# The keys' sums of squares dealt to partitions by a small DMA of ScalarE instead of identity matmuls, layer 0 attention

## The chip, the cores and the metric

The kernel runs on one core of a Trainium2 chip. The metric is the time of one execution on the device in microseconds. Three runs of the kernel before took 1753.96 to 1756.87 us, with a median of 1755.95 us.

## The reference, cut to what matters

The whole is two layers of gated cross attention and feed forward on 4 batches of 256 tokens of width 256. The change lies in layer 0's attention. There, each of 8 groups has one own key and value head and one context key and value head (128 wide), and 2 query heads for each of the two kinds:

```python
k = _fp8_linear_pertensor(ln_out, wk, wk_scale, k_in_scale).reshape(b, s, g, d)
k = _ln(k, kln_w, kln_b)                       # 256 own keys of a batch
kvx = jnp.einsum('bsi,oi->bso', cond, w_kv_x)
kx, vx = jnp.split(kvx, 2, axis=-1)
kx = _ln(kx.reshape(b, sc, g, d), kxln_w, kxln_b)   # 1601 context keys
scores = jnp.einsum('bsghd,btgd->bghst', q, k) * scale
p = jax.nn.softmax(scores, axis=-1)
```

So each of the 1601 + 256 = 1857 keys of a pair (group, batch) has a norm of its own, 1 / sqrt(its sum of squares over 128 + 128 * 1e-5). The kernel centres the weights beforehand, so that the mean is gone, and multiplies the scores by the norms, one number for each column of the score matrix, the same for all 128 queries (partitions).

## The kernel before, in words

The attention loop runs over 32 pairs (`NGB`); in iteration `it` the scores, softmax and values of pair `it` are computed in four blocks of 128 queries (`4 * it` to `4 * it + 3`), beside the projection of keys, values and queries of pair `it + 1`. The loop starts at -1, to fill. In the iterations 0 to 11 (`SPLITS` = 12) the engines also split the weights of a later group. Each engine has its own program, and all are in an order written out by hand; an engine waits only where a semaphore says so, and works strictly in its order.

TensorE's small products go through three PSUM banks by turns, in the order of `SLOTS` (line 801); `bank_of` and `wait_bank` give each product its bank and make it wait until the one three slots before has been read. The slots of one iteration: Q0, K0, K1, TQ0 (query transposes), K2, K3, Q1, SS (sums of squares), V0, ST (their transposes), V1, TQ1, V2, RS with V3 (the norms' transpose, in the free columns of V3's bank) and PR (output projection).

The path of the norms, before:

1. ScalarE writes the squares of the keys into `sq`, 128 x 1857, padded to 1872 = 16 x 117 (L1422).
2. TensorE, `squares` (L1632): four matmuls with a matrix of ones of 32 columns, each of 468 columns of `sq`, one to each quarter of the partitions of the bank.
3. ScalarE, `sums_out` (L1460): a copy to `sqs`.
4. TensorE, `turn_squares` (L1647): four fp32 transposes by the identity, 117 rows each.
5. VectorE, `squares_out` (L1197): takes one column of each quarter and adds the epsilon, to `ssc`, 117 x 16.
6. GpSimd, `key_norm` (L1054): to the power -0.5, to `rr`.
7. TensorE, `turn_norms` (L1720): one transpose, to 16 rows of 117.
8. ScalarE, `norms_out` (L1468): a copy of the 16 rows to `rsr`.
9. SP, `row_out` (L940): a DMA of the 16 rows to HBM, and `row_in` (L948): a DMA that reads the row back to all 128 partitions of `rsb` (in even iterations that buffer lies in the tile `x`).

VectorE needs the row in `scaled` (L1220) at the start of the next iteration, where it multiplies scores and norms and takes the maximum.

SP issues all DMAs of the loop: the weights of coming pairs, the small row and its broadcast, and eight transposing DMAs an iteration (`turn_p`, L962), which turn the probabilities for TensorE's `times_v` (L1765). A transposing DMA waits for VectorE's low part of the probabilities (`p_lo`, L1253) and GpSimd's own part (`split_self`, L1070).

Of the kernel before, what the change touches and what calls it, by code (L numbers as in the profile page):

```python
# [13 lines left out]
P = 128  # L14
# [36 lines left out]
SQG, SQT = 4, 4  # L51
SQW = (KC + SQG * SQT - 1) // (SQG * SQT)
SQN = SQG * SQT
RSC = SQN * SQW

BEFORE = 2 * STAGE + 2 * IC * WCOLS + 2 * RSC + 2 * SQT * SQW + 3 * 1024 + 2 * 2 * NQ * P + 2 * KCOLS + 2 * KTILES * D + 508
# [18 lines left out]
pa_full k_sq k_bias k_lo sums_out ssq_out kr_pow rst_out v_hi v_lo st_done mv_done rs_pow nm_done normed  # L75
# [30 lines left out]
def build(nc, A, out):  # L106
    m = Mem()
    whole = ExitStack()
    with whole:
# [5 lines left out]
        m.rs_d = nc.dram_tensor("rs_d", (2, SQN, SQW), F32, kind="Internal").ap()  # L115
# [9 lines left out]
def allocate(nc, m, whole):  # L125
# [14 lines left out]
    m.ones = sb(whole, "ones", [P, R], F32)  # L140
    m.rsmc = sb(whole, "rsmc", [P, 2 * G * HPG], F32)
# [11 lines left out]
    with ExitStack() as attn:  # L153
# [28 lines left out]
        with ExitStack() as c:  # L182
            m.stage = [sb(c, f"stage{i}", [P, STAGE], BF16) for i in range(2)]
            m.wsb = sb(c, "wsb", [P, 2 * IC * WCOLS], BF16)
            m.sq = sb(c, "sq", [P, RSC], F32)
            m.sqs = sb(c, "sqs", [P, SQT * SQW], F32)
# [6 lines left out]
            sb(c, "free_mid", [P, 254], F32)  # L193
# [15 lines left out]
            m.ssc = sb(c, "ssc", [P, SQN], F32)  # L209
            m.rr = sb(c, "rr", [P, 32], F32)  # L210
            m.rsr = sb(c, "rsr", [32, P], F32)
# [14 lines left out]
        with ExitStack() as c:  # L226
# [14 lines left out]
            m.wg = sb(c, "wg", [P, IC, NE], F32)  # L241
            m.brow = sb(c, "brow", [P, NE], F32)
# [304 lines left out]
def pool_prologue(e, m, s):  # L547
# [9 lines left out]
    e.memset(m.rr[:, :], 0.0).then_inc(s["p_pad"], 1)  # L557
    e.memset(m.sq[:, KC:RSC], 0.0).then_inc(s["p_pad"], 1)
# [234 lines left out]
def pe_prologue(e, m, s):  # L793
# [11 lines left out]
RS0 = 392  # L805
# [81 lines left out]
def wait_bank(e, s, it, what):  # L887
# [6 lines left out]
    if SLOTS[at] == ("PR",) and 0 <= it < LAG:  # L894
        at -= 3
# [3 lines left out]
    if before[0] == "Q":  # L899
        e.wait_ge(s["normed"], 2 * it + int(before[1]) + 1)  # L900
    elif before[0] == "K":
        e.wait_ge(s["k_lo"], 4 * it + int(before[1]) + 1)
    elif before[0] == "T":
        e.wait_ge(s["q_t32"], 2 * it + int(before[2]) + 1)
    elif before == "SS":
        e.wait_ge(s["sums_out"], it + 1)
    elif before == "ST":
        e.wait_ge(s["ssq_out"], it + 1)
    elif before[0] == "V":
        e.wait_ge(s["v_lo"], 4 * it + int(before[1]) + 1)  # L910
        if before == "V3":
            e.wait_ge(s["rst_out"], it + 1)
    else:
        e.wait_ge(s["acc_done"], it - LAG + 1)


def sp_attention(e, m, s):
# [22 lines left out]
    def row_out(it):  # L940
        if not it < NGB:
            return
        e.wait_ge(s["rst_out"], it + 1)
        if it >= 2:
            e.wait_ge(s[f"rs_in{it % 2}"], 16 * (it // 2))
        e.dma_start(m.rs_d[it % 2], m.rsr[0:SQN, 0:SQW]).then_inc(s["rs_row"], 16)

    def row_in(it):  # L948
# [10 lines left out]
        e.dma_start(m.rsb[it % 2], m.rs_d[it % 2].rearrange("t k -> (t k)").partition_broadcast(P)).then_inc(  # L959
# [17 lines left out]
    for it in range(-1, NGB + LAG - 1):  # L977
# [32 lines left out]
        row_out(it + 1)  # L1010
        if it < NGB:
# [3 lines left out]
        row_in(it + 1)  # L1015
# [13 lines left out]
def pool_attention(e, m, s):  # L1029
# [24 lines left out]
    def key_norm(it):  # L1054
        if not it < NGB:
            return
        e.wait_ge(s["ssq_out"], it + 1)
# [46 lines left out]
    for it in range(-1, NGB + LAG - 1):  # L1104
# [39 lines left out]
def dve_attention(e, m, s):  # L1144
# [51 lines left out]

    def squares_out(it):  # L1197
        if not it < NGB:
            return
        e.wait_ge(s["pa_full"], made(it, "ST"))  # L1200
        if it:
            e.wait_ge(s["kr_pow"], it)
        sums = bank_of(m, "ST")[0:SQW, :].rearrange("p (t g r) -> p g t r", t=SQT, g=SQG)[:, :, :, 0]
        e.tensor_scalar(m.ssc[0:SQW, :].rearrange("p (g t) -> p g t", g=SQG), sums, D * EPS5, None,  # L1204
                        ALU.add).then_inc(s["ssq_out"], 1)
# [91 lines left out]
    for it in range(-1, NGB + LAG - 1):  # L1297
# [53 lines left out]
        squares_out(it + 1)  # L1351
# [54 lines left out]
def act_attention(e, m, s):  # L1406
# [53 lines left out]
    def sums_out(it):  # L1460
# [7 lines left out]
    def norms_out(it):  # L1468
        if not it < NGB:
            return  # L1470
        e.wait_ge(s["pa_full"], made(it, "V3"))
        if it:
            e.wait_ge(s["rs_row"], 16 * it)
        e.copy(m.rsr[0:SQN, 0:SQW], bank_of(m, "RS")[0:SQN, RS0:RS0 + SQW]).then_inc(s["rst_out"], 1)

# [32 lines left out]
    for it in range(-1, NGB + LAG - 1):  # L1508
        if it == 0:
            e.wait_ge(s["p_pad"], 4)  # L1510
# [40 lines left out]
        sums_out(it + 1)  # L1551
# [28 lines left out]
        norms_out(it + 1)  # L1580
# [18 lines left out]
def pe_attention(e, m, s):  # L1599
# [32 lines left out]
    def squares(it):  # L1632
# [6 lines left out]
        if it == 0:  # L1639
            e.wait_ge(s["p_pad"], 2)  # L1640
# [4 lines left out]
        r.then_inc(s["pa_full"], 1)  # L1645

    def turn_squares(it):  # L1647
        if not it < NGB:
            return
        bank = bank_of(m, "ST")  # L1650
        wait_bank(e, s, it, "ST")
        e.wait_ge(s["sums_out"], it + 1)
        for t in range(SQT):
# [1217 lines left out]
```

## Time and profile before

| | |
|---|---|
| median of 3 runs | 1755.95 us (1753.96 to 1756.87) |
| profiled execution | 1757.05 us, span 1755.3 us |
| TensorE matmul busy | 1623.6 us, 92% of the span |
| VectorE, ScalarE, GpSimd busy | 80%, 79%, 72% |
| granted TensorE clock, mean | 0.974 |

A row of a timeline shows when an instruction (or a few of the same kind, "x4") started, counted from the span's start, and how long it took; in brackets stands how long its engine had been idle and what ended that. Matmuls overlap, so that the time a group takes in TensorE's order is read from its start to the start of the next group. A granted clock of 1.00 is TensorE's upper level. PE is TensorE, DVE VectorE, ACT ScalarE, POOL GpSimd, SP SyncE, and "SPq" is SP's queue, whose rows for a DMA give the time of the issue, not of the transfer. The loop's first iteration with scores begins near 100 us, its last products of keys and values end near 1165 us.

### The profile page before, as it was taken

To read this page: it belongs to the slowest core of one execution; us is meant where nothing else is said; L and a number is where in the kernel's file an instruction comes from. 1 tells how busy PE (TensorE), PEld (TensorE's weight loads), DVE (VectorE), ACT (ScalarE), POOL (GpSimd) and SP (SyncE) were. 2 spreads that over 40 slices of the span, in tenths; PEclk is the share of its full clock that TensorE was granted. 3 is DMA by queue.
4 is the path that set the end of the run, shared out by engine and by line. 5 is a ranking of instruction groups with operands and counts; after the bars stand their busy time and mean duration, and the time that the engine had idled before them with its cause. 6 is when DMAs were issued, how large, how long until landed. Compare 5 with 4: busy or idle time off the path is not lost. (4 is left out here: it accounts for less than half of the span.)

```text
span 1755.3 us, 43546 instructions
## 1 busy us (share of the span) xinstructions
PE 1623.6 (92%) x15989; PEld 1032.1 (59%) x16182; DVE 1405.2 (80%) x3479; ACT 1385.0 (79%) x2333; POOL 1272.2 (72%) x1171
## 2 busy tenths in 40 slices
PE   3389999999999999999999999998898999999997
PEld 1256776777677767777777777766553333333332
DVE  8879999999998898889988888888995755545322
ACT  4388888988887788778878887874346999999996
POOL 3646787787877876778777777775897989979500
PEclk9589999999999999999999999999999999999998
DMA  4269999999998889999999999997424222212100
GB/s 171 87 130 187 183 193 215 207 203 208 199 210 181 201 179 195 205 211 200 194 185 201 226 198 195 196 196 156 149 47 106 44 49 71 43 32 44 32 14 13
DMA packets 603173, 261.37 MB, mean 149 GB/s; under 512 B 568784, under 2 KB 575952, under 8 KB 601552
## 3 DMA queue, kind: packets, MB, share of 16 engines
q1 hardware_dynamic: 602960, 258.57, 70.7%
q8 instruction: 129, 2.11, 0.5%
q14 instruction: 84, 0.69, 0.1%
HBM read 99.15 MB, written 17.28 MB: 66 GB/s over the span
## 5 line engine op out<-in xcount | busy, mean ns | idle before, releaser
L1781 PE MATMUL pv<-PT,VV 128*128 128x256 bf16 (+1 forms) x2880 | 340.7, 275 | 7.7 <-DMA PT<-PB 7.6
L2351 POOL TENSOR_TENSOR l_rr<-l_rr,mhalf 128x32 f32<-128x32 f32 (+1 forms) x60 | 332.7, 5545 | 5.0
L1761 PE MATMUL score<-KK,QT 128*128 128x512 bf16 (+2 forms) x1795 | 315.5, 318 | 12.6 <-DVE mxp L1238 5.0
L1781 PEld LDWEIGHTS pv<-PT,VV 128*128 128x128 bf16 (+1 forms) x2880 | 280.7, 99 | 75.1 <-issue 33.7
L1505 ACT ACTIVATE PB<-S,rsum 128x1024 bf16<-128x1024 f32 (+1 forms) x256 | 246.3, 987 | 84.9 <-DVE rsum L1269 80.4
L1260 DVE SCALAR_TENSOR_TENSOR PB<-S,rsum,PB 128x1024 bf16<-128x1024 f32 (+1 forms) x256 | 302.4, 1182 | 1.9 <-ACT PB L1505 1.9
L1761 PEld LDWEIGHTS score<-KK,QT 128*128 128x128 bf16 x1920 | 159.7, 98 | 143.6 <-DVE mxp L1238 11.6
L1495 ACT ACTIVATE S<-S,nmx 128x1601 f32<-128x1601 f32 x128 | 209.8, 1639 | 10.2 <-DVE nmx L1250 10.1
L2617 ACT ACTIVATE P<-score 128x1024 f32<-128x1024 f32 x196 | 199.1, 1060 | 11.6 <-PE score L2709 5.9
L2729 PE MATMUL pv<-P,V 128*9 128x256 f32 (+1 forms) x2288 | 154.4, 385 | 2.8 <-ACT P L2617 2.2
L1621 PE MATMUL tb<-stage,wsb 128*128 128x512 bf16 x767 | 148.8, 337 | 5.5 <-DVE stage L624 4.1
L1079 POOL TENSOR_SCALAR S<-S,rsum 128x256 f32<-128x256 f32 x128 | 65.0, 508 | 115.1 <-DVE rsum L1269 102.8
L1062 POOL TENSOR_TENSOR rr<-ssc,mhalf 117x16 f32<-117x16 f32 x32 | 93.2, 2914 | 47.3 <-DVE ssc L1204 47.3
L1101 POOL TENSOR_TENSOR catq<-yt,ym 128x512 bf16<-128x512 f32 x64 | 120.6, 1884 | 0.3
L1238 DVE CUSTOM_DVE_ANT_0 S<-score,x 128x1024 f32<-128x1024 f32 (+1 forms) x128 | 104.5, 816 | 14.3 <-PE score L1761 11.8
L1238 DVE CUSTOM_DVE_ANT_0 S<-score,rsb 128x1024 f32<-128x1024 f32 (+1 forms) x128 | 104.5, 817 | 14.0 <-PE score L1761 9.8
L1621 PEld LDWEIGHTS tb<-stage,wsb 128*128 128x128 bf16 x768 | 67.0, 99 | 70.9 <-issue 8.7
L1035 POOL TENSOR_SCALAR a_nm<-a_mv 128x4 f32<-128x4 f32 x64 | 42.3, 661 | 89.8 <-DVE a_mv L1194 89.8
L1445 ACT ACTIVATE kn<-pa,a_nm,a_rs 128x128 f32<-128x128 f32 x256 | 95.9, 458 | 13.6 <-POOL a_nm L1040 13.6
L1417 ACT ACTIVATE KK<-tb,dcols 128x512 bf16<-128x512 f32 (+1 forms) x128 | 76.3, 596 | 37.0 <-PE tb L1621 35.8
L1083 POOL TENSOR_TENSOR PB<-S,PB 128x256 bf16<-128x256 f32 x128 | 96.6, 755 | 10.9
L1673 PE MATMUL tb<-wsb,stage 128*128 128x128 bf16 x1536 | 99.0, 222 | 4.5 <-DVE KK L1161 4.5
(271 smaller groups left out, 3627.7 us busy)
## 6 DMA issues: line engine op xcount, KB each, us to landing
x<-rs_d SPq DMA_DIRECT2D x16, 936.0 KB, 6.8
rsb<-rs_d SPq DMA_DIRECT2D x16, 936.0 KB, 5.5
wsb<-w_split SPq DMA_DIRECT2D x46, 256.0 KB, 4.5
wsb<-w_split SPq DMA_DIRECT2D x23, 512.0 KB, 5.4
wpr<-in_wprojT SPq DMA_DIRECT2D x23, 512.0 KB, 3.9
context_d<-stage SPq DMA_DIRECT2D x16, 400.2 KB, 3.7
l_ctx<-context_d SPq DMA_DIRECT2D x4, 1601.0 KB, 7.4
rawh<-in_w_all SPq DMA_DIRECT2D x12, 512.0 KB, 5.4
```

The source lines that it names most:

```text
L1101: e.tensor_tensor(out[:, :, pr * 256:(pr + 1) * 256], m.yt[:, :].rearrange("p (k c) -> p k c", k=2), m.ym[pr][:, :].rearrange("p (k c) -> ...
L1238: e.tensor_tensor_reduce(m.S32[par][:, at:at + b - a], m.score[:, a:b], m.rsb[it % 2][:, key:key + b - a], 1.0, start, ALU.mult, ALU.max, ...
L1260: e.scalar_tensor_tensor(m.PB[n % 2][:, lo:lo + b - a], m.S32[n % 2][:, a:b], m.rsum[n % 2][:, 1:2], m.PB[n % 2][:, 2 * a:a + b], ALU.mult ...
L1495: e.activation(x, x, ACT.Exp, bias=m.nmx[par][:, 1:2], accum_out=m.sums[par][:, 1:2])
L1505: e.activation(m.PB[n % 2][:, 2 * a:a + b], m.S32[n % 2][:, a:b], ACT.Copy, scale=m.rsum[n % 2][:, 1:2]).then_inc(s["p_hi"], 1)
L1621: r = e.matmul(bank[:, 0:b - a], wk[:, w, ic, D:2 * D], ctx_op(m, it, part, ic, a, b), start=(n == 0), stop=(n == 5))
L1673: r = e.matmul(bank[:, h * D:(h + 1) * D], ctx_op(m, it, part, ic, t * P, (t + 1) * P), wv[:, w, ic, D:2 * D], start=(n == 0), stop=(n == 5))
L1761: i = e.matmul(m.score[:, at:at + b - a], qt[:, kind, qp, q * P:(q + 1) * P], kk[:, kp, a:b], start=(k == 0), stop=(k == 2))
L1781: i = e.matmul(m.pv[:, at:at + 256], vv[0:rows, v, t, :], m.PT[k % 2][0:rows, turned(c, a), :], start=(c == first and r == 0), stop=(c == ...
L2351: e.tensor_tensor(rr, rr, m.mhalf[0:rows, 0:NH1], ALU.pow).then_inc(s["l1_rr"], 1)
L2617: e.activation(pr[:, :], bank, ACT.Exp, scale=float(D1) ** -0.5).then_inc(s["l1_exp"], 1)
L2729: r = e.matmul(m.pv[j * R:j * R + VC, 0:S], m.V1[p][0:rows, t, 4 * hq + j, :], probabilities(m, n, j // 2)[0:rows, at:at + S], start=(t == ...
```

## The change

The padded row gets another form: 1857 keys are padded to 1920 = 128 x 15. The four matmuls of the sums take 480 columns each. ScalarE's copy adds the epsilon, and ScalarE then waits for that copy and issues a DMA from four partitions of `sqs` (one of each quarter, 480 numbers) to all 128 partitions of `ssc` (15 numbers each). GpSimd raises these to the power -0.5, and SP sends `rr` (128 x 15) straight to HBM, of which the first 1872 numbers (`RSC`) are read back to all partitions, as before. The steps 4, 5, 7 and 8 above go, and with them the slots ST (left empty) and RS.

The order changes in three places: ScalarE takes the sums out ahead of the first part of the probabilities of block `4 * it + 1` (from iteration 0 on); GpSimd's `key_norm` comes after `split_self(4 * it + 1)`; SP's `row_in` comes directly behind `row_out`, ahead of the load of the projection's weights. Two small tiles (`wg`, `brow`) move to another place in SBUF, and the unused space is adjusted.

```diff
-SQG, SQT = 4, 4
-SQW = (KC + SQG * SQT - 1) // (SQG * SQT)
-SQN = SQG * SQT
-RSC = SQN * SQW
+SQG = 4
+SQC = (KC + P - 1) // P
+SQW = P * SQC // SQG
+RSC = KC + 15
...
-SLOTS = (("Q0",), ("K0",), ("K1",), ("TQ0",), ("K2",), ("K3",), ("Q1",), ("SS",), ("V0",), ("ST",), ("V1",), ("TQ1",),
-         ("V2",), ("RS", "V3"), ("PR",))
+SLOTS = (("Q0",), ("K0",), ("K1",), ("TQ0",), ("K2",), ("K3",), ("Q1",), ("SS",), ("V0",), (), ("V1",), ("TQ1",), ("V2",),
+         ("V3",), ("PR",))
...
-    if SLOTS[at] == ("PR",) and 0 <= it < LAG:
+    if not SLOTS[at] or SLOTS[at] == ("PR",) and 0 <= it < LAG:
         at -= 3
...
# SP
-        e.wait_ge(s["rst_out"], it + 1)
+        e.wait_ge(s["kr_pow"], it + 1)
         if it >= 2:
             e.wait_ge(s[f"rs_in{it % 2}"], 16 * (it // 2))
-        e.dma_start(m.rs_d[it % 2], m.rsr[0:SQN, 0:SQW]).then_inc(s["rs_row"], 16)
+        e.dma_start(m.rs_d[it % 2], m.rr[:, :]).then_inc(s["rs_row"], 16)
...
         row_out(it + 1)
+        row_in(it + 1)
         if it < NGB:
             load_projection(it - 1)
         if it == NGB - 1:
             load_projection(NGB - 1)
-        row_in(it + 1)
...
# GpSimd
-        e.wait_ge(s["ssq_out"], it + 1)
+        e.wait_ge(s["sums_in"], 16 * (it + 1))
         if it:
-            e.wait_ge(s["pa_full"], made(it - 1, "RS"))
-        else:
-            e.wait_ge(s["p_pad"], 1)
-        e.tensor_tensor(m.rr[0:SQW, 0:SQN], m.ssc[0:SQW, :], m.mhalf[0:SQW, 0:SQN], ALU.pow).then_inc(s["kr_pow"], 1)
+            e.wait_ge(s["rs_row"], 16 * it)
+        e.tensor_tensor(m.rr[:, :], m.ssc[:, :], m.mhalf[:, 0:SQC], ALU.pow).then_inc(s["kr_pow"], 1)
...
+        split_self(4 * it + 1)
         key_norm(it + 1)
         if it == -1:
             pool_round_end(e, m, s, 5)
-        split_self(4 * it + 1)
...
# ScalarE, sums_out
         if it:
-            e.wait_ge(s["pa_full"], made(it - 1, "ST"))
-        e.copy(m.sqs[:, :], bank_of(m, "SS")[:, 0:SQT * SQW]).then_inc(s["sums_out"], 1)
+            e.wait_ge(s["sums_in"], 16 * it)
+        e.activation(m.sqs[:, :], bank_of(m, "SS")[:, 0:SQW], ACT.Copy, bias=D * EPS5).then_inc(s["sums_out"], 1)
+        e.wait_ge(s["sums_out"], it + 1)
+        if it:
+            e.wait_ge(s["kr_pow"], it)
+        e.dma_start(m.ssc[:, :], m.sqs[0:SQG * R:R, :].rearrange("j (r c) -> j r c", c=SQC)).then_inc(s["sums_in"], 16)
...
# ScalarE, order of the loop
         exponentials(4 * it + 1)
         for b, i in SPLIT_AT.get(it, ())[0:1]:
             act_piece_high(e, m, s, b, i)
+        if it >= 0:
+            sums_out(it + 1)
         p_hi(4 * it + 1, 0)
         query_norm(it + 1, 1)
...
-        sums_out(it + 1)
+        if it == -1:
+            sums_out(0)
         values_high(it + 1, 0)
...
         values_high(it + 1, 2)
-        norms_out(it + 1)
         exponentials(4 * it + 2)
...
# TensorE, squares and order of the loop
-        w = SQT * SQW
         for j in range(SQG):
-            r = e.matmul(bank[j * R:(j + 1) * R, 0:w], m.ones[:, :], m.sq[:, j * w:(j + 1) * w], start=True, stop=True,
-                         skip_group_check=True)
+            r = e.matmul(bank[j * R:(j + 1) * R, 0:SQW], m.ones[:, :], m.sq[:, j * SQW:(j + 1) * SQW], start=True,
+                         stop=True, skip_group_check=True)
...
         values(it + 1, 0)
-        turn_squares(it + 1)
         scores(4 * it + 2, 1)
         values(it + 1, 1)
         turn_queries(it + 1, 1)
         values(it + 1, 2)
-        turn_norms(it + 1)
         values(it + 1, 3)
```

The functions `squares_out`, `norms_out`, `turn_squares` and `turn_norms` go as a whole, and so do the waits for them.

## Rows read from the trace of the kernel before

**Rows 1.** The page, DMA queues: packets, MB, share of 16 engines' span

```profile
q1 hardware_dynamic: 602960, 258.57, 70.7%
```

**Rows 2.** Busy times by stretch, the loop's first 12 iterations and the rest

```profile
core 0: us, PE busy (x) PEld busy (x) DVE busy (x) ACT busy (x) POOL busy (x), PEclk, DMA share, GB/s
140.20:526.50 386.30, 379.59 (x3432) 279.08 (x3477) 363.59 (x935) 331.74 (x673) 305.16 (x347) 1.00 0.98 201
526.50:1154.90 628.40, 621.00 (x5639) 461.27 (x5711) 559.92 (x1440) 508.91 (x920) 480.58 (x542) 1.00 0.97 198
```

**Rows 3.** Waits of TensorE in the whole span: total, times, longest

```profile
PE pv L1781 <- DMA PT<-PB: 7.6, 6, 2.7
...
PE tb L1726 <- POOL rr L1062: 1.3, 3, 0.5
...
PE pa L1654 <- ACT sqs L1466: 1.1, 3, 0.4
```

**Rows 4.** Timeline of TensorE in a second-half iteration: start, length, line

```profile
702.66 0.99 PE L1643 MATMUL tb<-sq,ones 128*32 128x468 f32 x8
...
705.90 1.50 PE L1673 MATMUL tb<-wsb,stage 128*128 128x128 bf16 x24
707.24 0.65 PE L1654 MATMUL pa<-ident,sqs 128*117 128x128 f32 x4
707.93 1.02 PE L1761 MATMUL score<-KK,QT 128*128 128x512 bf16 x8
...
710.13 0.61 PE L1717 MATMUL tb<-ident,kn 128*128 128x128 f32 x4
...
711.91 0.27 PE L1726 MATMUL tb<-ident,rr 117*32 117x117 f32 x1
712.02 0.61 PE L1681 MATMUL tb<-wsb,stage 128*128 128x128 bf16 x8
```

**Rows 5.** Timeline of ScalarE, the same stretch

```profile
703.51 1.15 ACT L1505 ACTIVATE PB<-S,rsum 128x1024 bf16<-128x1024 f32 x1 [0.23 <-DVE rsum L1269]
704.57 1.49 ACT L1445 ACTIVATE kn<-pa,a_nm,a_rs 128x128 f32<-128x128 f32 x4
705.94 0.56 ACT L1466 COPY sqs<-tb 128x468 f32<-128x468 f32 x1
707.44 0.59 ACT L1432 CAST VV<-tb 128x512 bf16<-128x512 f32 x1 [0.94 <-PE tb L1673]
```

**Rows 6.** Timelines of VectorE and GpSimd, the same stretch

```profile
708.05 0.69 DVE L1174 TENSOR_TENSOR VV<-tb,VV 128x512 bf16<-128x512 f32 x1
...
710.95 0.69 DVE L1174 TENSOR_TENSOR VV<-tb,VV 128x512 bf16<-128x512 f32 x1 [0.79 <-ACT VV L1432]
...
708.17 2.90 POOL L1062 TENSOR_TENSOR rr<-ssc,mhalf 117x16 f32<-117x16 f32 x1 [2.04 <-DVE ssc L1204]
```

**Rows 7.** DMA issues of lines 974 and 946 from 300 to 1100 us (ns), and SP's timeline

```profile
L974 SPq DMA_TRANSPOSE PT<-PB x184: 1296/2440/5573, 299.5 to 1098.5; - x184
...
DMA to landing us min/median/max: 4.0/5.0/10.0
...
L946 SPq DMA_DIRECT2D rs_d<-rsr x23: 317/326/529, 328.4 to 1096.2; - x23
...
DMA to landing us min/median/max: 1.3/1.8/2.8
...
704.29 6.72 SPq L974 DMA_TRANSPOSE PT<-PB  x3
713.27 0.32 SPq L946 DMA_DIRECT2D rs_d<-rsr  x1
...
714.92 0.32 SPq L959 DMA_DIRECT2D x<-rs_d  x1
```

**Rows 8.** Timelines in a first-half iteration: ScalarE, VectorE, TensorE

```profile
323.25 0.59 ACT L1432 CAST VV<-tb 128x512 bf16<-128x512 f32 x1 [0.42 <-PE tb L1673]
...
303.52 0.08 DVE L1238 DVE_READ_ACCUMULATOR2_ANT mxp<- 128x1 f32 x1
...
303.66 1.47 PE L1761 MATMUL score<-KK,QT 128*128 128x512 bf16 x6
```

More of the change, by code:

```diff
@@ L74 @@
 ld_k ld_q ld_v ld_xq rs_row rs_in0 rs_in1
-pa_full k_sq k_bias k_lo sums_out ssq_out kr_pow rst_out v_hi v_lo st_done mv_done rs_pow nm_done normed
+pa_full k_sq k_bias k_lo sums_out sums_in kr_pow v_hi v_lo st_done mv_done rs_pow nm_done normed
 q_hi q_t32 q_lo pw_in pw_last pw_hi pw_lo acc_done
@@ L140, in allocate @@
     m.ones = sb(whole, "ones", [P, R], F32)
+    m.wg = sb(whole, "wg", [P, IC, NE], F32)
+    m.brow = sb(whole, "brow", [P, NE], F32)
     m.rsmc = sb(whole, "rsmc", [P, 2 * G * HPG], F32)
@@ L184, in allocate @@
             m.wsb = sb(c, "wsb", [P, 2 * IC * WCOLS], BF16)
-            m.sq = sb(c, "sq", [P, RSC], F32)
-            m.sqs = sb(c, "sqs", [P, SQT * SQW], F32)
+            m.sq = sb(c, "sq", [P, SQG * SQW], F32)
+            m.sqs = sb(c, "sqs", [P, SQW], F32)
             m.kn = [sb(c, f"kn{i}", [P, 512], F32) for i in range(2)]
@@ L192, in allocate @@
             vv[0] = sb(c, "VV0", [P, 2, KTILES, D], BF16)
-            sb(c, "free_mid", [P, 254], F32)
+            sb(c, "free_mid", [P, 194], F32)
             qt[1] = sb(c, "QT1", [P, 2, 2, NQ * P], BF16)
@@ L208, in allocate @@
             m.anm = [sb(c, f"a_nm{i}", [P, 4], F32) for i in range(2)]
-            m.ssc = sb(c, "ssc", [P, SQN], F32)
-            m.rr = sb(c, "rr", [P, 32], F32)
-            m.rsr = sb(c, "rsr", [32, P], F32)
+            m.ssc = sb(c, "ssc", [P, SQC], F32)
+            m.rr = sb(c, "rr", [P, SQC], F32)
             m.mxp = [sb(c, f"mxp{i}", [P, 1], F32) for i in range(2)]
@@ L556, in pool_prologue @@
     i.then_inc(s["rank_done"], 1)
-    e.memset(m.rr[:, :], 0.0).then_inc(s["p_pad"], 1)
-    e.memset(m.sq[:, KC:RSC], 0.0).then_inc(s["p_pad"], 1)
+    e.memset(m.sq[:, KC:SQG * SQW], 0.0).then_inc(s["p_pad"], 1)
     e.wait_ge(s["mhalf_done"], 1)
@@ L1195, in query_stats @@
         mv.then_inc(s["mv_done"], 1)
[L1197 to L1205, printed above, removed]
     def projected(i):
@@ L1464, in sums_out @@
         if it:
-            e.wait_ge(s["pa_full"], made(it - 1, "ST"))
-        e.copy(m.sqs[:, :], bank_of(m, "SS")[:, 0:SQT * SQW]).then_inc(s["sums_out"], 1)
[L1468 to L1471, printed above, removed]
+            e.wait_ge(s["sums_in"], 16 * it)
+        e.activation(m.sqs[:, :], bank_of(m, "SS")[:, 0:SQW], ACT.Copy, bias=D * EPS5).then_inc(s["sums_out"], 1)
+        e.wait_ge(s["sums_out"], it + 1)
         if it:
-            e.wait_ge(s["rs_row"], 16 * it)
-        e.copy(m.rsr[0:SQN, 0:SQW], bank_of(m, "RS")[0:SQN, RS0:RS0 + SQW]).then_inc(s["rst_out"], 1)
+            e.wait_ge(s["kr_pow"], it)
+        e.dma_start(m.ssc[:, :], m.sqs[0:SQG * R:R, :].rearrange("j (r c) -> j r c", c=SQC)).then_inc(s["sums_in"], 16)
     def projection_high(i):
@@ L1509, in act_attention @@
         if it == 0:
-            e.wait_ge(s["p_pad"], 4)
+            e.wait_ge(s["p_pad"], 3)
             e.wait_ge(s["w_lo_dve"], 16)
@@ L1639, in squares @@
         if it == 0:
-            e.wait_ge(s["p_pad"], 2)
-        w = SQT * SQW
+            e.wait_ge(s["p_pad"], 1)
         for j in range(SQG):
-            r = e.matmul(bank[j * R:(j + 1) * R, 0:w], m.ones[:, :], m.sq[:, j * w:(j + 1) * w], start=True, stop=True,
-                         skip_group_check=True)
[L1645 to L1653, printed above, removed]
-            r = e.transpose(bank[0:SQW, t * P:(t + 1) * P], m.sqs[:, t * SQW:(t + 1) * SQW], m.ident[:, :])
+            r = e.matmul(bank[j * R:(j + 1) * R, 0:SQW], m.ones[:, :], m.sq[:, j * SQW:(j + 1) * SQW], start=True,
+                         stop=True, skip_group_check=True)
         r.then_inc(s["pa_full"], 1)
@@ L1661, in values @@
         bank = bank_of(m, f"V{i}")
-        if i < 3:
-            wait_bank(e, s, it, f"V{i}")
+        wait_bank(e, s, it, f"V{i}")
         if i == 0:
@@ L1718, in turn_queries @@
         r.then_inc(s["pa_full"], 1)
-    def turn_norms(it):
-        if not it < NGB:
-            return
-        bank = bank_of(m, "RS")
-        wait_bank(e, s, it, "RS")
-        e.wait_ge(s["kr_pow"], it + 1)
-        e.transpose(bank[0:R, RS0:RS0 + SQW], m.rr[0:SQW, :], m.ident[0:SQW, 0:SQW]).then_inc(s["pa_full"], 1)
     def project(i):
@@ L1940, in pe_turn_tokens @@
         e.wait_ge(s["v_lo"], 4 * NGB)
-        e.wait_ge(s["rst_out"], NGB)
     elif k == 2:
```

16 lines of the change are left out of this document (4 added, 12 removed).

## The prediction, made before the changed kernel ran

> **What bounds the kernel now.** I read the page for its DMA queue first [rows 1], then the busy times by stretch, then the waits of TensorE, and only then the timelines of one iteration. In the attention loop's second half (526.5 to 1154.9 us) it is busy 621.0 of 628.4 us, in its first half (140.2 to 526.5 us) 379.6 of 386.3, both at a granted clock of 1.00, the upper level (2.4 GHz) [rows 2]. VectorE stands at 559.9 of 628.4 in the second half (89%) but at 363.6 of 386.3 in the first (94%); ScalarE at 81% and 86% [rows 2]. So inside the loop a microsecond of TensorE's own work is a microsecond of time, unless another engine has less room than what is saved, and that can only be so in the first half. The waits of TensorE agree: at the two groups that go, it waited 1.1 and 1.3 us in the whole run, and for the transposed probabilities 7.6 us [rows 3]. The iteration shown starts its squares at 702.66 us.
>
> **TensorE, removed.** The four transposes of the sums start at 707.24, the next matmul group (scores) at 707.93: 0.69 us of the order of work. The one transpose of the norms starts at 711.91, the values' last piece at 712.02: 0.11 us, though the row gives its own length as 0.27, since it overlaps its neighbours [rows 4]. Together 0.80 us an iteration. **Added:** the squares' sums run over 480 columns in place of 468. Their eight records last 0.99 us, so 12/468 of that, 0.02 us. Net 0.78 us.
>
> **VectorE and ScalarE, removed.** VectorE's small addition (117 by 16) and ScalarE's copy of the 16 rows both go. Both engines have idle time right behind them (VectorE 0.79 us at 710.95 [rows 6]), so I count them as nothing; they are room in hand.
>
> **ScalarE, added and moved.** The copy of the sums (0.56 us) comes before the probabilities' first part and the four query norms instead of after them, and carries the DMA issue behind it. TensorE's squares end at 703.65 (702.66 + 0.99) [rows 4]; ScalarE's exponentials are done before 703.51, where it starts the part after an idle 0.23 us [rows 5]. So the copy runs 703.7 to 704.3. Then it waits for its own result and issues the transfer. No DMA is issued by ScalarE in this trace, so I bound the issue from both sides: 0.32 us is the plain DMA on SP (the row's minimum 317 ns, maximum 529), and 2.44 us is the median of a transposing one on the same queue, 5.57 its longest [rows 7]. I take 0.32, since the nearest row is that of a plain DMA of the same small row; with 0.1 us for the wait on itself (an estimate: a bit more than twice the 0.04 us from the end of TensorE's V0, 705.90 + 1.50 [rows 4], to its copy at 707.44 [rows 5]) ScalarE is free at 704.7. The probabilities' part, which started at 703.51, starts 1.2 us later; the four norms then end at 707.2 in place of 706.06 [rows 5]. What hides this: until now the copy (0.56) and an idle 0.94 us before the values' copy at 707.44 followed [rows 5], and that copy waits for TensorE's V0, which isn't moved. Who waits for the norms: TensorE's query transposes at 710.13, after the change 709.44 [rows 4]: 2.2 us of room. They also need V0's low part out of their bank, done at 708.74 (708.05 + 0.69) [rows 6]: 0.7 us of room, plus the 0.2 us that ScalarE is early at V0. So an issue of up to 0.32 + 0.9 = 1.2 us costs TensorE nothing in this iteration; beyond that each microsecond costs one.
>
> **The transfer and the row behind it.** Landing is bounded by 1.3 us (the least of the small row to HBM, 1.8 in the median) and 10.0 us (the longest of a transposed block, 5.0 in the median) [rows 7]. I take 3 us, nearest the small one: 704.6 to 707.6. GpSimd's power, on it, ran from 708.17 to 711.07 after 2.04 us of idling for VectorE's sums [rows 6]. In the new order GpSimd first does the own-keys split, which fits into that idle time (its inputs have long been there), and starts the power at about 707.9: 15 columns by 2.90/16 each make 2.72 us, done at 710.6. The row's DMA, at 713.27 until now behind TensorE's transpose and ScalarE's copy, goes at 710.7, the broadcast at about 712.7 instead of 714.92 [rows 7]. SP's queue: the projection's load is moved behind the broadcast, and the transposes of the second probability half stand behind both; all of them get earlier. The transfer may land 2.2 us later than I take it (5.2 us in all) before even the row is later than now. The wait for the earlier round's row is met an iteration before. The broadcast stays at 1872 numbers. The added small packets load the DMA engines: 602,960 packets took 70.7% of 16 engines' 1755 us, 33 ns each [rows 1]; some 256 small ones in place of 16 are 0.5 us an iteration for each engine. TensorE hardly waits for DMA, so I cost it at nothing; if the cover were gone it would be that 0.5 us, 15 us in all.
>
> The trace gives 1.8 us for a transfer whose 16 rows lie on as many partitions [rows 7]. The Trainium skill, "DMA: Bandwidth & Descriptors", section "Why a DMA increments its semaphore by 16 and not by 1", states that a DMA is spread over the largest number of engines, at most 16, that divides the slowest dimension of both sides. Here these are 4 and 128, so four engines would take 32 packets each; by the 33 ns above that is an estimated 1.1 us on top of 1.8. By the row alone the landing is at 1.8 us, by the rule at 2.9, and the sum is the same by both, since 5.2 would be hidden.
>
> **What is late next.** In the second half: VectorE idles 0.79 us for V1's copy alone [rows 6], so it keeps up with 0.78 us. I take all of it: 19 iterations by 0.78 are 14.8 us. In the first 12 (those that also split weights) ScalarE ends its weight work at 322.83 and then idles 0.42 us for V1 at 323.25 [rows 8]; with V1 0.69 us earlier it is ScalarE that is late, so V1's copy moves by about 0.5. From there VectorE works nearly without a gap into the next iteration, where TensorE's scores at 303.66 start just after VectorE's last read at 303.52 + 0.08 [rows 8]. So those iterations follow V1's copy: 12 by 0.5 are 6.0 us. The fill iteration ahead of the loop has long stalls of its own: nothing. The waits at the two groups [rows 3], 2.4 us, go in part: 1.2. Sum 22.0 us. Profiled execution: 1757.05 us (span 1755.3 and 1.75 around it) minus 22.0 is 1735.05. It lies 1.1 us above the median of the runs, 1755.95, so in the median's terms 1734.
>
> **The rivals.**
> Something else holds part of it: VectorE, at 94% in the first half, gives nothing there, and the 0.5 us of packets shows in some of the rest. For: the tight step at 303.66. Against: VectorE loses work as well. First half 0 (6.0 us less), second half 19 by 0.5 in place of 0.78 (5.3 less): 1745.
> ScalarE's issue is held up. At 704.29, just when it issues, SP starts three transposing DMAs, 6.72 us [rows 7]. If ScalarE's is held for as long as the shorter of them lasts (1.3 to 1.5 us, so 1.5), the second half loses 0.3 of its 0.78 us (19 by 0.48 are 9.1 gained), while in the first half all of 1.2 us over my 0.32 comes through, 12 by (1.2 - 0.5) are 8.4 lost; with the waits' 1.2 that is 2 us gained: no change that can be told, 1754. This is the case within 0.2%. The skill's same page, section "Issuing engines are not separate DMA queues", states that they all run on the same 16 engines and interleave, and that only the sequencer's time is saved; it puts no price on waiting. No run here shows it.
> The other side, slower: the same place at the median price of a transpose, 2.44 us. Second half: 2.44 is 1.24 over the free 1.2, minus 0.78 leaves 0.46 lost, by 19 are 9 us; first half 2.1 - 0.5 = 1.6 by 12, 19 us; less the waits' 1.2 that is plus 27, 1783. It decides from an issue of about 1.6 us on. For it: the transposes really meet it every iteration. Against: plain DMAs on SP take 0.32 to 0.53 us even right behind transposes. A landing near 10 us would do it too, over the row: power at 714.6, row 717.3, broadcast 719.2, more than 4 us later than now.
> That the change doesn't do what it says (the sums not needed by TensorE any more, but its banks still waited for): the values' third bank now waits for the query norms of Q1, done before; I give it nothing.
>
> **How the numbers follow.** Forecast 0.57 (1734, its own range 1727 to 1741: below, 31 by 0.80 and all waits, 28 us; above, two thirds of the 22 us), part held 0.14 (1745), no change 0.11 (1754), slower 0.18 (1783 and up). A measurement can tell 0.2%, 3.5 us, from no change. Faster 0.71, same 0.11, slower 0.18. The range 1726 to 1762 leaves out most of the slower case and little below.
>
> **What would show it.** Right: iterations of the second half at 33.8 to 33.9 us; no transposes between V0 and the scores; ScalarE's gap between the sums' copy and the next part under 0.6 us; GpSimd's power starting before V0's low part ends; the row's DMA some 2.5 us earlier. Wrong: a gap of over 1.5 us on ScalarE behind the copy, the query transposes waiting for VectorE's V0 part, GpSimd idling for the small transfer past 710 us of such an iteration, or TensorE idle in front of the scores for VectorE's maximum in every iteration.

## The result, and the profile after

The changed kernel takes 1736.43 us (median of 4 runs, 1733.42 to 1740.90) against 1756.07 us (4 runs) for the kernel before: ratio 0.9888, 95% interval 0.9872 to 0.9904. So the gain is 19.6 us, with 1734 forecast and a range from 1726 to 1762. The profiled execution took 1734.62 us (span 1732.8), 22.4 less than the profiled one of before.

The busy times of the two parts of the loop, which answer to [rows 2] (same stretches of the clock, so a little more work falls into each):

```profile
140.20:526.50 386.30, 381.16 (x3500) 278.27 (x3498) 363.03 (x931) 333.65 (x668) 310.92 (x351) 1.00 0.96 203
526.50:1154.90 628.40, 624.04 (x5714) 458.56 (x5712) 560.33 (x1444) 513.08 (x917) 502.09 (x552) 1.00 0.98 201
```

TensorE seems nearer to full than before (624.0 of 628.4 us against 621.0), but this difference comes from the records. The trace of the kernel before lacks 125 matmuls of the scores (1795 are recorded for 1920 weight loads), and this trace of the changed kernel lacks none. A second trace of the same changed kernel (the run `e0_after` below) lacks as many and shows 620.0 of 628.4. What can be said is that in a plain second-half iteration (one without an extra wait) of the complete trace TensorE has no idle time. First this trace, then the incomplete one of the same kernel:

```profile
900.00:934.06 34.06, 34.06 (x315) 25.04 (x313) 29.87 (x80) 27.92 (x51) 27.16 (x30) 1.00 1.01 205
...
692.18:726.24 34.06, 33.85 (x312) 25.05 (x312) 29.85 (x80) 28.05 (x51) 27.19 (x31) 1.00 0.98 189
```

TensorE's timeline of such an iteration, answering to [rows 4]:

```profile
692.18 1.01 PE L1621 MATMUL tb<-sq,ones 128*32 128x480 f32 x8
...
695.44 1.50 PE L1640 MATMUL tb<-wsb,stage 128*128 128x128 bf16 x24
696.78 1.24 PE L1720 MATMUL score<-KK,QT 128*128 128x512 bf16 x9
...
699.19 0.61 PE L1684 MATMUL tb<-ident,kn 128*128 128x128 f32 x4
...
726.24 1.01 PE L1621 MATMUL tb<-sq,ones 128*32 128x480 f32 x8
```

The next squares start 34.06 us later; before, it was 34.62 us (the squares' starts at 702.66 [rows 4] and 737.28). So a second-half iteration is 0.57 us shorter (34.62 to 34.05, in nearly all of them). A first-half one is 0.53 us shorter (34.94 to 34.41, again the commonest values). From the first squares to the last, the loop is 17.9 us shorter in the profiled pair: 10.2 us over the last 18 intervals, 8.8 over the 12 before them (2.8 of these in the one right behind the fill), and the fill itself 1.1 us longer. The 2.8 us are no sure gain of the change: that one interval took 37.8 us before and 35.0 after, but from 36.7 to 37.7 in five of the later variants of the changed kernel, and 35.9 in the kernel before with more transposes. The remaining 4.5 us of that pair lie behind the last squares. That part isn't touched by the change, and over the profiles of this case it took between 595.4 and 601.6 us, without relation to the kernel. So the totals of single executions can differ by some 6 us from there alone, and the size of an effect is better read from the iterations than from the totals.

ScalarE and its queue, SP's queue and GpSimd in the same iteration, answering to [rows 5], [rows 7] and [rows 6]; "ACTq" is the issue of the DMA:

```profile
693.26 0.57 ACT L1447 ACTIVATE sqs<-tb 128x480 f32<-128x480 f32 x1 [0.47 <-PE tb L1621]
693.86 0.53 ACTq L1451 DMA_DIRECT2D ssc<-sqs  x1
694.50 1.15 ACT L1482 ACTIVATE PB<-S,rsum 128x1024 bf16<-128x1024 f32 x1 [0.66 <-ACT sqs L1447]
695.55 1.49 ACT L1426 ACTIVATE kn<-pa,a_nm,a_rs 128x128 f32<-128x128 f32 x4
...
693.80 8.36 SPq L968 DMA_TRANSPOSE PT<-PB  x3
702.25 0.53 SPq L940 DMA_DIRECT2D rs_d<-rr  x1
704.47 0.32 SPq L953 DMA_DIRECT2D x<-rs_d  x1
...
695.74 0.48 POOL L1071 TENSOR_SCALAR S<-S,rsum 128x256 f32<-128x256 f32 x1
696.29 1.49 POOL L1073 CAST PB<-S 128x256 bf16<-128x256 f32 x1
697.86 0.67 POOL L1075 TENSOR_TENSOR PB<-S,PB 128x256 bf16<-128x256 f32 x1
698.49 2.75 POOL L1054 TENSOR_TENSOR rr<-ssc,mhalf 128x15 f32<-128x15 f32 x1
```

The issue on ScalarE takes 0.53 us and leaves a gap of 0.66 us, although SP starts its three transposing DMAs 0.06 us ahead of it. Here GpSimd doesn't wait for the transfer: its split of the own keys fills the time until 698.49. In the 31 iterations with scores it waited once, 2.5 us, when the power started only 7.2 us behind the issue.

### The profile page after: what moved, and what is told of

Its sections match the earlier page's. It is cut to its first block and busy times, and to the rows that moved or that the text cites. A ratio compares the mean times of both kernels' runs of the same rounds, so it can differ in the third digit from the quotient of the medians.

```text
span 1732.8 us, 43279 instructions
## 1 busy us (share of the span) xinstructions
PE 1619.0 (93%) x16022; PEld 1014.7 (59%) x16022; DVE 1389.3 (80%) x3447; ACT 1377.3 (79%) x2301; POOL 1284.1 (74%) x1170
## 5 line engine op out<-in xcount | busy, mean ns | idle before, releaser
L1720 PE MATMUL score<-KK,QT 128*128 128x512 bf16 (+2 forms) x1920 | 341.9, 322 | 6.2 <-DVE mxp L1220 5.0
L1242 DVE SCALAR_TENSOR_TENSOR PB<-S,rsum,PB 128x1024 bf16<-128x1024 f32 (+1 forms) x256 | 295.4, 1154 | 4.6 <-ACT PB L1482 4.5
L1600 PE MATMUL tb<-stage,wsb 128*128 128x512 bf16 (+1 forms) x768 | 150.3, 339 | 4.8 <-DVE stage L623 4.1
L1083 POOL TENSOR_TENSOR yt<-yq,ym 128x512 f32<-128x512 bf16 x64 | 95.9, 1498 | 13.9 <-DVE ym L1276 9.5
L1426 ACT ACTIVATE kn<-pa,a_nm,a_rs 128x128 f32<-128x128 f32 x256 | 95.5, 454 | 12.3 <-POOL a_nm L1034 12.3
L2664 PE MATMUL score<-QB,KT 32*128 32x256 bf16 (+1 forms) x1110 | 93.6, 275 | 7.3 <-ACT P L2572 4.8
```

Of the source, the lines that this page charges most:

```text
L1242: e.scalar_tensor_tensor(m.PB[n % 2][:, lo:lo + b - a], m.S32[n % 2][:, a:b], m.rsum[n % 2][:, 1:2], m.PB[n % 2][:, 2 * a:a + b], ALU.mult ...
L1600: r = e.matmul(bank[:, 0:b - a], wk[:, w, ic, D:2 * D], ctx_op(m, it, part, ic, a, b), start=(n == 0), stop=(n == 5))
L1720: i = e.matmul(m.score[:, at:at + b - a], qt[:, kind, qp, q * P:(q + 1) * P], kk[:, kp, a:b], start=(k == 0), stop=(k == 2))
L2664: r = e.matmul(bank[0:rows, at:at + S], m.KT1[p][j * R:(j + 1) * R, hq, t * P:t * P + rows], m.QB[p][j * R:(j + 1) * R, hq, :], start=True ...
```

## The experiments

The iterations given are the distances from one start of the squares to the next, as in the rows above.

**The changed kernel again,** without an edit.

> The changed kernel once more, beside the others of this call. Its first four executions spread from 1733.4 to 1740.9 us, so its gain is known only to about 3 us. Both theories below say 19 to 22 us under the kernel before (the iterations of the second half were 0.57 us shorter in its profile, those of the first half 0.53). If its iterations are the same and the total differs again by some microseconds, the spread lies outside the attention loop.

Measured: 1738.07 us against 1756.89, ratio 0.9891 [0.9875, 0.9907], with the same iterations of 34.05 us. The experiments below are compared with this run. The later ones did not run beside it, so their distances in us to the changed kernel are uncertain by 3 to 6 us.

This trace lacks matmul records, and the profiled one of the result doesn't. The same stretch of the same kernel reads, first in this trace, then in that one:

```profile
695.05 1.50 PE L1640 MATMUL tb<-wsb,stage 128*128 128x128 bf16 x24
696.61 1.02 PE L1720 MATMUL score<-KK,QT 128*128 128x512 bf16 x8
...
695.44 1.50 PE L1640 MATMUL tb<-wsb,stage 128*128 128x128 bf16 x24
696.78 1.24 PE L1720 MATMUL score<-KK,QT 128*128 128x512 bf16 x9
```

Where the scores have 8 records they seem to start 1.56 us behind the group before them, and where they have 9, 1.34 us.

**The four transposes twice, in the kernel before.**

```diff
-        for t in range(SQT):
+        for t in (*range(SQT), *range(SQT)):
             r = e.transpose(bank[0:SQW, t * P:(t + 1) * P], m.sqs[:, t * SQW:(t + 1) * SQW], m.ident[:, :])
```

> The kernel before, with the four transposes of the sums issued twice. Theory A (the bound is TensorE's order; my 0.69 us for the four was too large by one score matmul, 0.21 us, whose record is missing in that trace, so that the four are worth 0.44 to 0.48 us): second-half iterations of 35.06 to 35.11 us in place of 34.62, in all 14 to 15 us more than before, about 1770. Theory B (the four are worth 0.69 us as I read it, and 0.21 us of the gain are lost again to a wait in the changed kernel): 35.3 us, 21 us more, 1777. Theory C (the gain comes from the shorter path of the norms and from the new order, not from TensorE's work): under 3 us more.

Measured: 1765.54 us, ratio 1.0049 [1.0037, 1.0062] to the kernel before. The squares of two successive iterations on TensorE:

```profile
916.30 0.99 PE L1643 MATMUL tb<-sq,ones 128*32 128x468 f32 x8
...
951.35 0.99 PE L1643 MATMUL tb<-sq,ones 128*32 128x468 f32 x8
```

The two shown are 35.05 us apart; the commonest value is 35.06, 0.44 more than 34.62. So four more transposes cost 0.44 us, not 0.69: theory A, as to the iteration. Its total was too high. The first-half iterations of 34.94 us got 0.44 us longer, but the mean over the 11 behind the first was only 0.27, and the fill and the iteration behind it got shorter, hence 9 us in all instead of 14.

**Five transposes back, in the changed kernel.**

```diff
         wait_bank(e, s, it, f"V{i}")
+        if i == 2:
+            for t in range(4):
+                e.transpose(bank[0:117, t * P:(t + 1) * P], m.ident[:, 0:117], m.ident[:, :])
+            e.transpose(bank[0:R, 0:117], m.ident[0:117, 0:R], m.ident[0:117, 0:117])
```

> The changed kernel, with five fp32 transposes of the identity, of the shapes of those that went, put back on TensorE ahead of the values' third group, into a bank that this group overwrites: no other engine reads them, and no wait comes with them. Theory A: 0.54 to 0.58 us an iteration come back, 17 to 18 us, nearly the time of the kernel before (about 1753), second-half iterations at 34.6. Theory B: 0.80 us, but 0.21 us of wait are covered then, so the same. Theory C: within 3 us of the changed kernel.

Measured: 1748.04 us, ratio 0.9954 [0.9942, 0.9967]. Timeline of TensorE:

```profile
905.97 1.01 PE L1621 MATMUL tb<-sq,ones 128*32 128x480 f32 x8
...
940.57 1.01 PE L1621 MATMUL tb<-sq,ones 128*32 128x480 f32 x8
```

Second-half iterations of 34.59 us: 0.54 of the 0.57 us are back, by TensorE's work alone. In the first half 34.59 too, 0.18 more than 34.41, since there TensorE had a wait that took in the rest. So of the total only 10 us came back, not 17. The other 9 us of the gain stayed. In part that follows from where the transposes were put: behind V1, so that V1 was still early and only TensorE's own order got longer. With the transposes at their old place the first half wasn't tested.

**The three moves undone.**

```diff
# ScalarE: behind query_norm(it + 1, 1), as before
-        if it >= 0:
-            sums_out(it + 1)
...
+        sums_out(it + 1)
         values_high(it + 1, 0)
# GpSimd
+        key_norm(it + 1)
...
         split_self(4 * it + 1)
-        key_norm(it + 1)
# SP: row_in(it + 1) behind load_projection again
```

> The changed kernel with its three moves undone: ScalarE takes the sums out and issues after the query norms, GpSimd's power comes ahead of its own-keys split, SP's broadcast comes behind the projection's load. Theory A: the moves only give room; the row is some 2 us later than in the changed kernel, which was not waited for: within 3 us of the changed kernel, second-half iterations at 34.05 to 34.1. Theory C: the moves carry the gain, 10 us or more are lost. A rival within A: GpSimd now waits for the small transfer with the split behind it, the transposing DMA of the second probability half is late, and TensorE waits for it: 0.3 us or more an iteration.

Measured: 1778.51 us, ratio 1.0123 [1.0109, 1.0137]: 40 us over the changed kernel and 22 over the kernel before. My theory A was wrong by 37 us. Waits from 530 to 1130 us (total, times, longest), and then the timelines of one iteration (squares at 647.75) on ScalarE's queue, GpSimd and VectorE:

```profile
POOL rr L1054 <- DMA ssc<-sqs: 68.2, 17, 5.7
DVE S L1220 <- POOL PB L1075: 38.7, 17, 3.8
...
PE score L1717 <- DVE mxp L1220: 15.8, 14, 2.3
...
651.76 0.55 ACTq L1451 DMA_DIRECT2D ssc<-sqs  x1
...
655.65 2.74 POOL L1054 TENSOR_TENSOR rr<-ssc,mhalf 128x15 f32<-128x15 f32 x1 [4.32 <-DMA ssc<-sqs]
...
659.53 0.67 POOL L1075 TENSOR_TENSOR PB<-S,PB 128x256 bf16<-128x256 f32 x1
...
660.23 1.22 DVE L1220 CUSTOM_DVE_ANT_0 S<-score,rsb 128x1024 f32<-128x1024 f32 x1 [2.18 <-POOL PB L1075]
```

The transfer is there 3.9 us behind its issue. GpSimd waits 4.3 us with the split behind it in its order, the split ends 12.4 us behind the squares, and VectorE, which may overwrite that score tile only then, is 2.2 us late; TensorE waits for its maximum in the end. The two runs that follow undo one move each. SP's move wasn't undone alone, and no run has the other two undone without it; in this run the broadcast of the iteration shown still starts 12.1 us behind the squares, against 12.3 in the changed kernel.

**ScalarE's move alone undone** (the first part of the diff above).

> The changed kernel, where only ScalarE's part goes back to its old place (behind the query norms). The transfer was seen to land about 3.5 us after its issue, which is now 2.6 us later, so GpSimd waits some 1.5 us for it, but with its own-keys split already done. Theory D (the 40 us of the old order come from one chain: late transfer, GpSimd waiting for it with the split stuck behind, VectorE waiting for the split before it may overwrite the probabilities): nothing of that chain is left, within 3 us of the changed kernel, second-half iterations at 34.05 to 34.1, GpSimd waiting 1 to 2 us each. Theory E (the place on ScalarE alone costs, since the later parts of the probabilities get late): 10 us or more over the changed kernel.

Measured: 1740.54 us, ratio 0.9909 [0.9877, 0.9940]; second-half iterations of 34.05 us in 9 of 18 cases, GpSimd waiting:

```profile
POOL rr L1054 <- DMA ssc<-sqs: 26.8, 16, 3.3
```

Five first-half iterations that take 34.41 us in the changed kernel take 34.13 to 34.22 here. So the new place of ScalarE's copy costs something in the first half, which I haven't explained.

**GpSimd's move alone undone** (the second part).

> The changed kernel, where only GpSimd's power goes back ahead of the own-keys split. Theory D: the transfer is issued early and lands 3.5 us later, near 697.4 in an iteration whose squares start at 692.2; the power then ends near 700.2 and the split near 701.9, that is 9.7 us after the squares, against 10.7 in the kernel before, where nobody waited. So within 5 us of the changed kernel, second-half iterations at 34.05 to 34.3. Rival F (GpSimd's order alone makes the 40 us): most of them appear here, iterations near 35.2.

Measured: 1743.59 us, ratio 0.9923 [0.9895, 0.9951]; 34.05 us too in most of the second half. GpSimd waits 30.3 us in 16 cases from 530 to 1130 us, but for an early transfer, so in most iterations the split is still in time (VectorE waits for it five times, 7.7 us in all). With one of the two moves undone, 2 and 6 us over the changed kernel are left of the 40, and the intervals of both runs overlap that of the changed kernel. That is what theory D says: one chain, which each of these two moves cuts.

**A second issue on ScalarE.**

```diff
         e.dma_start(m.ssc[:, :], ...).then_inc(s["sums_in"], 16)
+        if it == NGB - 1:
+            return
+        if it:
+            e.wait_ge(s["spare"], 16 * it)
+        e.dma_start(m.scr[:, 0:SQC], m.sqs[0:SQG * R:R, :].rearrange("j (r c) -> j r c", c=SQC)).then_inc(s["spare"], 16)
```

> The changed kernel, with a second DMA of the same form behind the first on ScalarE, into a spare tile that nobody reads. It takes some 0.55 us more of ScalarE's time at the same place (the issue took 0.53 to 0.58 us there). By the prediction's step (up to 1.2 us of issue are free in the second half, none in the first): second-half iterations unchanged at 34.05, first-half ones 0.4 to 0.55 us longer, in all 5 to 7 us. Rival: the issue has no room in either half, 17 us more. Other rival: the issue is a mere gap that the other engines hide everywhere, under 1 us.

Measured: 1743.91 us, ratio 0.9914 [0.9884, 0.9944], 6 us over the changed kernel, which the total alone wouldn't show clear of its spread. The iterations do: the second half stays at 34.05 us, as forecast, and the first half is 6.1 us longer in sum. Nine of its twelve iterations got longer, by 0.1 to 1.1 us. One of them, at 34.41 in the changed kernel, takes 35.27:

```profile
278.98 1.01 PE L1627 MATMUL tb<-sq,ones 128*32 128x480 f32 x8
...
314.25 1.01 PE L1627 MATMUL tb<-sq,ones 128*32 128x480 f32 x8
```

**The power twice on GpSimd.**

```diff
+        e.tensor_tensor(m.scr[:, 0:SQC], m.ssc[:, :], m.mhalf[:, 0:SQC], ALU.pow)
         e.tensor_tensor(m.rr[:, :], m.ssc[:, :], m.mhalf[:, 0:SQC], ALU.pow).then_inc(s["kr_pow"], 1)
```

> The changed kernel, with the power computed twice on GpSimd, first to a spare tile: the row and all behind it on GpSimd come 2.75 us later. By the prediction's step (room of about 2.2 us up to the old place of the row, and none of TensorE's waits on it even there) the time hardly moves: 0 to 0.3 us an iteration, at most 9 us in all. Rival (the earlier row and the earlier GpSimd work carry part of the gain): 0.5 us or more an iteration, 15 us and more.

Measured: 1770.47 us, ratio 1.0075 [1.0044, 1.0106], 32 us over the changed kernel: the rival. The row itself got late in some iterations: VectorE waited for its broadcast in 5 of the 17 from 530 to 1130 us, 8.2 us in all. In a plain one it did not (the row's DMA at 938.05, squares at 925.85), and that one is 0.44 us longer all the same: what stands behind the power on GpSimd has a price that I had not seen. VectorE and GpSimd of this run:

```profile
938.21 1.08 DVE L1272 TENSOR_SCALAR yq<-yq 128x512 bf16<-128x512 bf16 x1
939.32 0.58 DVE L1274 TENSOR_SCALAR ye<-yq 128x512 int16<-128x512 int16 x1
939.94 1.20 DVE L1277 TENSOR_SCALAR ym<-ye 128x512 int16<-128x512 int16 x1
...
937.99 1.15 POOL L1084 TENSOR_TENSOR yt<-yq,ym 128x512 f32<-128x512 bf16 x1
939.09 0.67 POOL L1043 CAST QT<-t 128x512 bf16<-128x512 f32 x1
939.84 1.16 POOL L1045 TENSOR_TENSOR QT<-t,QT 128x512 bf16<-128x512 f32 x1
```

In the changed kernel GpSimd is done with these at 704.57, and the same three of VectorE follow in 0.29 us each:

```profile
703.41 1.16 POOL L1045 TENSOR_TENSOR QT<-t,QT 128x512 bf16<-128x512 f32 x1
...
704.54 0.29 DVE L1271 TENSOR_SCALAR yq<-yq 128x512 bf16<-128x512 bf16 x1
704.87 0.29 DVE L1273 TENSOR_SCALAR ye<-yq 128x512 int16<-128x512 int16 x1
705.19 0.29 DVE L1276 TENSOR_SCALAR ym<-ye 128x512 int16<-128x512 int16 x1
```

Three 0.29 us instructions take 2.9 us when they run against GpSimd's. The inverse sums on VectorE and ScalarE's next part stand behind them, and TensorE waits 0.26 us for VectorE's maximum in this iteration (34.49 us), up to 1.5 in the first half. How the 32 us divide between this and the late row wasn't tested.

**SP issues the small transfer**, ahead of its transposing DMAs, and in another run behind two of them.

```diff
# SP
+        if it >= 0:
+            deal_out(it + 1)      # the waits and the dma_start that stood on ScalarE
         turn_p(4 * it, 1)
         turn_p(4 * it, 0)
# ScalarE issues only the first one itself
...
```

> The changed kernel, where from iteration 0 on SP issues the small transfer instead of ScalarE, ahead of its transposing DMAs of that stretch (the very first one stays on ScalarE). ScalarE loses the 0.66 us between the copy of the sums and the next part. Theory G (the issue on ScalarE costs only where ScalarE has no room, the first half; in the second TensorE has no idle time left): first-half iterations 0.15 to 0.25 us shorter (34.2 to 34.3), second-half ones still 34.05, in all 2 to 3 us under the changed kernel, about 0.987 of the kernel before. Rival H: the transposing DMAs come 0.5 us later and the transfer lands later among them, GpSimd waits for it, and 3 us or more are lost. This is also the version that could beat both.

> The same, but with SP's issue behind two transposing DMAs, each of which holds SP's queue for 1.5 to 4 us. The transfer is then issued some 4 to 5 us later and lands near 10 to 11 us behind the start of the squares; the power and all behind it on GpSimd are 3 to 4 us late, more than in the run with the second power. Theory G: as there or worse, 0.4 to 1.3 us an iteration, 15 to 40 us over the changed kernel. Rival: only the row is late, and it has room since the broadcast is needed 12 us later: under 5 us.

Measured ahead: 1736.93 us, 0.9897 [0.9878, 0.9915], no difference to the changed kernel; behind: 1764.58 us, 1.0042 [1.0009, 1.0074]. Of theory G the run with the late issue is as forecast (27 us over the changed kernel, GpSimd waiting 52.9 us in 16 cases). The first half of the other is not: its iterations stay at 34.42 instead of 34.2 to 34.3, so ScalarE's 0.66 us had cost nothing there either. The issue of the same transfer on SP is of the same length as on ScalarE (from 530 to 1130 us, ns, least, median, most):

```profile
L940 SPq DMA_DIRECT2D ssc<-sqs x17: 561/567/582, 556.3 to 1105.6; - x17
```

**The values' third part ahead of the weight work,** in the order of ScalarE and VectorE.

```diff
# ScalarE; VectorE's values_low(it + 1, 2) moves in the same way
+        values_high(it + 1, 2)
         if 0 <= it < SPLITS:
             act_weights_high(e, m, s, it // 2 + 2, 3 * (it % 2))
         if 0 <= it < SPLITS and it % 2 == 0:
             act_centre_weights(e, m, s, it // 2 + 2)
-        values_high(it + 1, 2)
```

> The changed kernel, where in the first-half iterations ScalarE and VectorE do the values' third part before the weight work of that slot instead of after it. Theory I (what keeps the first half at 34.42 instead of 34.05 us is the stretch from V1 over ScalarE's 3.4 us of query and weight work to V2's low part on VectorE, behind which VectorE has no idle time until TensorE waits for its maximum): the first-half iterations lose 0.1 to 0.35 us each, second-half ones stay at 34.05, in all 1 to 4 us. Rival J: VectorE's total work is the limit there, whatever its order: the first half stays at 34.42 or gets longer.

Measured: 1736.50 us, 0.9881 [0.9859, 0.9904]. Four of the first-half iterations that stood at 34.41 now take 34.05:

```profile
279.67 1.01 PE L1621 MATMUL tb<-sq,ones 128*32 128x480 f32 x8
...
313.72 1.01 PE L1621 MATMUL tb<-sq,ones 128*32 128x480 f32 x8
```

So the place was right for these four (theory I). But the one behind the fill took 37.7 us in place of 35.0, where TensorE waited 3.0 us for a transposed probability instead of 1.9, two of the second half got longer too, and the total doesn't move.

**Both together:** this order, and the small transfer issued by SP ahead of its transposing DMAs.

> The run before together with SP's issue ahead of its transposing DMAs. With SP's issue alone the first half stayed at 34.42 us. Theory I: once the values' third part no longer waits, the 0.66 us on ScalarE may show: 0 to 0.1 us an iteration less than in the run before, not measurable in the total (under 1.5 us). Rival J: no difference to the changed kernel.

Measured: 1735.90 us, 0.9876 [0.9853, 0.9899], the same again, as its rival J has it for the total, though three first-half iterations are at 34.05. No version of these beats the changed kernel by more than the spread.

## Why the prediction was right

**TensorE is the bound** held in the second half: the complete trace has no idle time left in its plain iterations, and 0.54 of 0.57 us come back with the transposes alone.

**The size of the removed work** is the term that was off: net 0.78 us, where 0.57 was measured. In all that is 14.8 us forecast for the second half and 10.2 measured; 0.8 us of that difference is that I counted 19 iterations, and there are 18 distances. I read the four transposes from the start of their group to the start of the scores' [rows 4], 0.69 us. But that scores' group has 8 matmuls in the row and 9 in the changed kernel. One of them, 0.21 us, has no record, and so the group seemed to start late. The two traces of the changed kernel show it without any transposes: 1.56 us with 8 records, 1.34 with 9. 0.69 - 0.21 is 0.48, and the doubling measured 0.44. The single transpose, 0.11, was about right (0.54 - 0.44 = 0.10).

**The first half** came out at 0.53 us an iteration with 0.5 forecast, and 6.0 us over 11 iterations. The twelfth, behind the fill, added 2.8 us that no step of mine explains and that most variants of the changed kernel don't repeat. For the mechanism, that these iterations follow V1's path over ScalarE to VectorE, the run with the values ahead of the weight work speaks, in four iterations; the run with ScalarE's move undone says that the path isn't the whole of it. My reason for 0.5 was wrong: I let V1 come 0.69 us earlier and ScalarE hold it back to 0.5. V1 came only some 0.48 us earlier, and ScalarE's idle 0.42 was all but enough for that. Two errors met in the right figure, which is luck. There was also just enough room for one issue: the second one shows in most first-half iterations.

**ScalarE's issue** took 0.53 us in place of 0.32, with the gap at 0.66 in place of 0.4. That was within the room of 1.2 us that I had worked out for the second half. With the second issue the gap is 1.26 us and more and the iteration still 34.05, so the room is at least that. The rivals of a held-up issue fall: the least and the median in the run are 529 and 548 ns, and only the first of all took 1093.

**The transfer** takes 4.1 us in the median to where GpSimd can use it, 2.4 to 5.5 in the 31 waits of the old order (taken: 3), in time but for the once in the changed kernel, in an iteration of 34.50 us. The Trainium skill, "DMA: Bandwidth & Descriptors", section "Why a DMA increments its semaphore by 16 and not by 1", states besides the number of engines that each of them ends its share with a write to the semaphore. This can be checked on the page's queue row of the changed kernel:

```profile
q10 hardware_dynamic: 4224, 0.25, 0.2%
```

That is 132 packets for each of 32 transfers, 128 of data and 4 more, one for each of four engines; by that rule, the trace agrees.

**The row behind it** was a wrong step that cost nothing. I had the power start before V0's low part ends and the row's DMA and the broadcast go 2.5 and 2.2 us earlier. The power starts 6.31 us behind the squares (before: 5.51) and 0.2 us after V0's low part has ended. The split ahead of it took 2.75 us, its cast alone 1.49, where I had let it fit into 2.04. Then SP's transposing DMAs hold the queue to 702.16. So the row's DMA goes 10.07 us behind the squares (before: 10.61), and the broadcast 12.29 (before: 12.26), not earlier at all. Of my five signs of being right only one came true as written, the transposes gone; the iteration (34.05 for 33.8 to 33.9) and ScalarE's gap (0.66 for under 0.6) missed narrowly, the power's start and the row's DMA clearly. The signs of being wrong stayed away, except that GpSimd did wait once, and TensorE's query transposes three times for VectorE (7.4 us), as they had before the change (5.7).

**"The three moves only give room"** was not a step of the prediction, but what it implied, and what I expected of the old order. The price lies in what GpSimd does next (the split), and, 2.75 us later than now, in GpSimd's larger work running against VectorE. So my "2.2 us of room" for the transfer can't be used as it stands: it looked at the row alone. A power that ended 2.75 us later cost 32 us, and a transfer issued behind two transposing DMAs 27.

**The total** then: 1734 forecast, 1736.4 and 1738.1 measured. For the profiled pair I had 22.0 us and 22.4 were measured, but that closeness is luck. The loop gave 17.9: 4.6 us less than forecast in the second half, 2.8 more in the first, 1.1 lost in the fill, and the 1.2 us for the waits at the two groups, which I can't find apart from the iterations. The other 4.5 us lie behind the loop, where nothing was changed. The lower end of my own range had a slip: 31 by 0.80 and 2.4 are 27.2 us, not 28.

## What to carry to other kernels

Where TensorE is the bound, taking small matmuls off it pays what they take in its order, but compare the matmul and weight-load counts of the neighbouring group before trusting a distance between two starts, or the busy time of two traces. A small transfer in place of them trades 0.5 us of TensorE for some 4 us of latency, and nearly 8 at worst here: what may stand behind its wait on the consuming engine is work that nobody needs within those 4 us, and it is cheaper to do other work first than to wait. An engine's position in time can have a price of its own, beside what it produces.

## What the runs showed that was not expected

VectorE's 16-bit `TENSOR_SCALAR` instructions can be held up by GpSimd's: in the rows of the run with the second power 0.29 us became 0.58 to 1.20 us, and each ended about 0.15 us after a GpSimd instruction did. The Trainium skill, "SBUF — State Buffer", section "Who interferes with whom", says that the two engines share one pair of ports as an exclusive lock, which blocks whoever comes second for the whole instruction of the other, and names `tensor_scalar` among VectorE's that can take it. These rows agree. The power of the same run doesn't: while it runs on GpSimd, VectorE's three take their 0.29 us, and so the measurement decides that not every GpSimd instruction blocks them.

```profile
185.12 2.75 POOL L1055 TENSOR_TENSOR rr<-ssc,mhalf 128x15 f32<-128x15 f32 x1
...
186.74 0.29 DVE L1272 TENSOR_SCALAR yq<-yq 128x512 bf16<-128x512 bf16 x1
187.06 0.29 DVE L1274 TENSOR_SCALAR ye<-yq 128x512 int16<-128x512 int16 x1
187.39 0.29 DVE L1277 TENSOR_SCALAR ym<-ye 128x512 int16<-128x512 int16 x1
```

And the DMA to 128 short destinations has an issue of 0.53 to 0.58 us on ScalarE and on SP alike, where that of the 16-row block took 0.32 [rows 7].
